# A scatter into an adjacency matrix: two fp16 weight parts instead of three bf16, groups written out, marks in another order

## The chip, the core and the metric

The kernel runs on one core of one Trainium2 chip. A core has five engines with queues of their own: TensorE (PE in the profile, with its weight loads as PEld), VectorE (DVE), ScalarE (ACT), GpSimd (POOL, "PoolE" in the change's words) and SyncE (SP, which issues DMAs). They meet through semaphores alone. The metric is the device time of one launch in microseconds (us); lower is better.

## The reference, cut to what matters

The network works on 625 nodes with 512 features and 20,000 edges that are sorted by destination. Four layers follow each other; the first two need matrices that are made from the edge list:

```python
# layer 0: a weighted graph convolution with self loops of weight 1
deg  = segment_sum(concat([edge_weight, ones(n)]), dst_f)
dinv = where(deg > 0, rsqrt(deg), 0)
agg  = segment_sum(h[src_f] * (dinv[src_f] * w * dinv[dst_f])[:, None], dst_f) + b_conv
# layer 1: a mean over incoming edges; layers 2 and 3: attention over the same edges
agg  = segment_sum(x[src], dst);  mean = agg / maximum(deg, 1)
```

The kernel never gathers rows. It builds, once, a dense matrix of edge counts and one of edge weights (source by destination) and uses them as matmul operands in all layers.

## The kernel before, in words

The node axis is padded to NP = 640, five tiles of 128. The edge list is cut into NG = 40 groups of 512 edges, each group as CH = 4 chunks of 128 edges, one edge to a partition. Since the edges are sorted, a group's destinations fall into a window of WIN = 34 columns (more passes would follow if they did not; the outer loop `Fori(0, passes + 1)` runs once here).

**The stretch before the scatter** loads and transposes the edge lists, finds each group's first destination (`base_f`), normalises x tile by tile (`first_norm`, `first_stats`, `first_rest`) and multiplies it with the first weights (L1838 on PE). `step(...)` on DVE makes the next DVE instruction wait for this one. DVE splits the edge weights into three bf16 parts (`w_part`, L2564 to L2567), whose sum is the float32 weight.

**The scatter**, for each group g, uses buffer b = g % HOT with HOT = 4:

- DVE writes source marks: for chunks 0 to 2, `hot_src[b][:, j]` is 1 where the node number (`iota16`) equals the edge's source, 628 wide (`marks`, L2590). Chunk 3 is made by ACT in two instructions, the distance |node - source| (L1724) and relu(1 - distance) (L1726).
- DVE writes destination marks for all four chunks in one instruction, 4 x 34 wide (L2595), between the second and the third source mark. Its two tensor inputs, `iota16` and `dst_rel` (a part of the tile `edge_col`), are both in SBUF.
- POOL multiplies the destination marks with the three weight parts, 3 x 4 x 34 = 408 wide (L1511).
- PE, for each of 4 chunks and 5 source tiles, loads the 128 source marks as weights and does three matmuls into PSUM: marks and first part together (68 columns, L2134), then the second and third part (34 columns each, L2137). That is 60 matmuls to a group. The increment of `scat_full` tells that the group's sums are there.
- DVE adds the sums into the window of the matrix (`add`, L2605). The window's place comes from `base_i` by a register load on DVE's sequencer (L2601).

DVE's order is hot(g + 3), add(g): it marks three groups ahead. `hot(g + 4)` waits until PE has done group g. The loops over groups are hardware loops (`Fori`) of four groups a turn, on DVE, ACT, POOL and PE, with group numbers in registers. After the scatter DVE sums features (L2642) and the degrees, and ACT and DVE split the matrix into high and low parts (L1729, L2629).

Of the kernel before, what the change touches and what calls it, by code (L numbers as in the profile page):

```python
# [40 lines left out]
ACCW = NP + ROOM  # L41

# [147 lines left out]
def build(nc, a, out):  # L190
    ctx = ExitStack()
    with ctx:
        def sb(name, shape, dt):
            return ctx.enter_context(nc.sbuf_tensor(name, shape, dt))
# [24 lines left out]
        w_part = sb("w_part", [P, 3, CH, NG], BF16)  # L219
        hot_dst = sb("hot_dst", [P, HOT, CH, 4 * ROOM], BF16)  # L220
# [32 lines left out]
        src_col, dst_rel, w_col = [edge_col[:, i * CH * NG:(i + 1) * CH * NG].rearrange("p (j g) -> p j g", j=CH) for i in range(3)]  # L253
        l3s = edge_col[:, 0:5 * NT * NJ].rearrange(
# [27 lines left out]
        hot_src = [m[:, :, :].rearrange("p t n -> p (t n)").bitcast(BF16)[:, b * CH * NP:(b + 1) * CH * NP].rearrange(  # L282
            "p (j n) -> p j n", j=CH) for m in (mask, z) for b in range(2)]
        hot_abs = [mask[:, NT - 1, :].bitcast(BF16)[:, b * NP:(b + 1) * NP] for b in range(2)]
# [1111 lines left out]
        def _(g):  # L1396
# [108 lines left out]
            with g.Fori(0, passes + 1) as kp:  # L1505
                with g.Fori(0, NG // HOT) as gi:
                    for b in range(HOT):
                        gr = gi * HOT + b
                        c = kp * NG + gr + 1
                        g.wait_ge(hot_dst_up, c)  # L1510
                        g.tensor_tensor(hot_dst[:, b, :, WIN:4 * WIN].rearrange("p j (i n) -> p i j n", i=3),  # L1511
                                        hot_dst[:, b, :, 0:WIN].unsqueeze(1).broadcast_to([P, 3, CH, WIN]),
                                        w_part[:, :, :, bass.ds(gr, 1)].broadcast_to([P, 3, CH, WIN]), ALU.mult).then_inc(hot_w_up, 1)
# [157 lines left out]
        def _(act):  # L1671
# [29 lines left out]
            act.activation(diag, ident[:, :].unsqueeze(1).broadcast_to([P, NT - 1, P]), ACT.Copy).then_inc(acc_up, 1)  # L1701
            act.activation(w_acc[:, NT - 1, (NT - 1) * P:NP], ident[:, :], ACT.Copy).then_inc(acc_up, 1)
# [16 lines left out]
            with act.Fori(0, passes + 1) as kp:  # L1719
                with act.Fori(0, NG // HOT) as gi:  # L1720
                    for b in range(HOT):
                        g = gi * HOT + b
                        act.wait_ge(scat_full, kp * NG + g + 1)
                        act.activation(hot_abs[b % 2][:, 0:NW], iota16[:, 0:NW], ACT.Abs, bias=src_col[:, CH - 1, bass.ds(g, 1)], scale=-1.0).then_inc(hot_abs_up, 1)  # L1724
                        act.wait_ge(hot_abs_up, kp * NG + g + 1)
                        act.activation(hot_src[b][:, CH - 1, 0:NW], hot_abs[b % 2][:, 0:NW], ACT.Relu, bias=1.0, scale=-1.0).then_inc(hot_act_up, 1)  # L1726
# [329 lines left out]
        def _(pe):  # L2056
# [8 lines left out]
            pe.matmul(bflat(BIG0["base"])[:, 0:2 * NG], ones[0:NG, :], xn[0:NG, 0, 0:2 * NG],  # L2065
# [53 lines left out]
            with pe.Fori(0, passes + 1) as kp:  # L2119
                with pe.Fori(0, NG // HOT) as gi:  # L2120
                    for b in range(HOT):
# [6 lines left out]
                        for j in range(CH):  # L2128
                            for t in range(NT):
                                s = hot_src[b][:, j, t * P:(t + 1) * P]  # L2130
                                o = t * 2 * WIN


                                pe.matmul(to[:, o:o + 2 * WIN], s, hot_dst[:, b, j, 0:2 * WIN],  # L2134
                                          start=(j == 0 and t == 0), stop=False, skip_group_check=True)
                                for i in (2, 3):
                                    ins = pe.matmul(to[:, o + WIN:o + 2 * WIN], s, hot_dst[:, b, j, i * WIN:(i + 1) * WIN],  # L2137
                                                    start=False, stop=(j == CH - 1 and i == 3), skip_group_check=True)
# [323 lines left out]
        def _(dve):  # L2462
# [33 lines left out]
            step(dve.tensor_scalar(xn[0:NG, 0, NG:2 * NG], ident[0:NG, 0:NG], mnmx[0:NG, 2:3], None, ALU.mult))  # L2496
            def tile_sums(slot, src):
                dve.bn_stats(stats[:, slot, :], src).then_inc(st_up, 1)  # L2498
# [35 lines left out]
            for name, to in (("src", src_col), ("w", w_col)):  # L2534
# [4 lines left out]
            step(dve.tensor_copy(base_f[:, :], bflat(u)[:, 0:NG]))  # L2539
            first_norm(0)  # L2540
# [4 lines left out]
                              base_f[:, :].unsqueeze(1).broadcast_to([P, CH, NG]), ALU.subtract).then_inc(big_read, 1)  # L2545
            first_stats(2)
            first_norm(1)
            dve.wait_ge(big_read, u + 1)
# [15 lines left out]
            step(dve.tensor_copy(w_part[:, 0, :, :], w_col[:, :, :]))  # L2564
            for i in (1, 2):
                step(dve.tensor_tensor(w_col[:, :, :], w_col[:, :, :], w_part[:, i - 1, :, :], ALU.subtract))
                ins = dve.tensor_copy(w_part[:, i, :, :], w_col[:, :, :])  # L2567
                if i == 1:
                    step(ins)
            ins.then_inc(w_ready, 1)  # L2570
# [14 lines left out]
            with dve.Fori(0, passes + 1) as kp:  # L2585
                def hot(g, b):

                    dve.wait_ge(scat_full, kp * NG + g + 1)
                    def marks(j):
                        return dve.tensor_scalar(hot_src[b][:, j, 0:NW], iota16[:, 0:NW], src_col[:, j, bass.ds(g, 1)], None, ALU.is_equal)  # L2590

                    marks(0)
                    marks(1)

                    dve.tensor_tensor(hot_dst[:, b, :, 0:WIN], iota16[:, 0:WIN].unsqueeze(1).broadcast_to([P, CH, WIN]),  # L2595
                                      dst_rel[:, :, bass.ds(g, 1)].broadcast_to([P, CH, WIN]), ALU.is_equal).then_inc(hot_dst_up, 1)
                    marks(2).then_inc(hot_src_up, 1)

                def add(g, b):

                    w0 = dve.value_load(base_i[0:1, bass.ds(g, 1)], min_val=0, max_val=NP)  # L2601
# [3 lines left out]
                    dve.tensor_tensor(win, scat(b).rearrange("p (t c n) -> p t c n", t=NT, c=2), win, ALU.add).then_inc(scat_read, 1)  # L2605
# [3 lines left out]
                for b in range(HOT - 1):  # L2609
                    hot(b, b)  # L2610
                wait_apart(dve, pass_up, kp * 3 + 1)
                with dve.Fori(0, NG // HOT - 1) as gi:
                    for b in range(HOT):
                        hot(gi * HOT + b + HOT - 1, (b + HOT - 1) % HOT)
                        add(gi * HOT + b, b)
                hot(NG - 1, HOT - 1)
                dve.wait_ge(hot_dst_up, kp * NG + NG)
                dve.tensor_scalar(dst_rel[:, :, :], dst_rel[:, :, :], float(WIN), None, ALU.subtract).then_inc(pass_up, 1)
                dve.tensor_scalar(base_f[0:1, :], base_f[0:1, :], float(WIN), float(NP), ALU.add, ALU.min).then_inc(pass_up, 1)
                for b in range(HOT):  # L2620
                    add(NG - HOT + b, b)
# [34 lines left out]
            dve.tensor_scalar(degs[:, 0, :], degree, 1.0, None, ALU.add).then_inc(deg_up, 1)  # L2656
# [161 lines left out]
```

## Time and profile before

| | |
|---|---|
| median of 3 runs | 871.7 us (870.86 to 872.49) |
| the profiled execution | 873.27 us, of which the span of its instructions is 871.3 us |
| busy, share of the span | PE 95%, PEld 83%, DVE 72%, POOL 57%, ACT 53% |
| granted TensorE clock, mean | 0.994 |
| before the scatter (0 to 28.07 us) | 28.07 us |
| the scatter (DVE's first mark to the end of its last add) | 28.07 to 102.83 us |
| all that follows | 768.47 us |

All numbers below come from this one profiled execution, and times of instructions are counted from the span's start. The busy share of PE counts overlapping matmuls of some 190 ns that start every 28 ns, so it tells little here; starts tell more. An instruction can start before the recorded end of the one ahead of it on its engine.

### The profile page before, as it was taken

The page shows a single profiled execution, that of the slowest core. Times are in us where ns is not written, and L with a number is a line of the kernel's source. Part 1 is how long each engine was busy: PE and PEld are TensorE (multiplying, and loading weights), DVE is VectorE, ACT ScalarE, POOL GpSimd, SP SyncE. Part 2 cuts the span into 40 slices and gives each one's busy share as a digit, 9 for nine tenths or more (in the row PEclk, how much of TensorE's full clock was granted, in tenths as well). Part 3 has the DMA queues.
Part 4 walks back from the last instruction along what each step waited for, and adds up shares of the span by engine and source line. Part 5 has one row for each costly group of instructions (what it writes and reads, how often), then busy time and mean ns, then how long its engine had stood idle before and what let it go on. Part 6 is the DMA issues. An engine that isn't in the chain of part 4 may idle for free.

```text
span 871.3 us, 18208 instructions
## 1 busy us (share of the span) xinstructions
PE 823.4 (95%) x6778; PEld 725.1 (83%) x6778; DVE 628.2 (72%) x1271; ACT 458.2 (53%) x773; POOL 494.3 (57%) x542
## 2 busy tenths in 40 slices
PE   3999989999999999999999999999999999999896
PEld 2999867889998879999887989887998978875565
DVE  7998878974676673576766467677348766699996
ACT  5988675344771343575233467333347633256673
POOL 7454573578433577542556943266674339457971
PEclk9999999999999999999999999999999999989999
DMA  6000102133000152200124410014230003100111
GB/s 163 2 0 0 38 25 87 41 94 122 25 1 13 41 158 73 72 14 1 29 68 126 110 49 2 13 31 121 86 95 13 1 1 85 37 1 32 48 60 60
DMA packets 49761, 44.34 MB, mean 51 GB/s; under 512 B 6014, under 2 KB 37440, under 8 KB 49699
## 3 DMA queue, kind: packets, MB, share of 16 engines
q1 hardware_dynamic: 47234, 39.72, 15.7%
q10 hardware_dynamic: 2464, 3.80, 1.6%
q8 instruction: 38, 0.62, 0.3%
q14 instruction: 25, 0.20, 0.1%
HBM read 42.04 MB, written 1.33 MB: 50 GB/s over the span
## 4 chain that ended last, share of the span: by engine, by line
PE 73%; DVE 15%; ACT 4%; issue 3%; DMA 2%; DVEq 1%; POOL 1%; SPq 0%; ACTq 0%
PE psum L1832 20%; PE psum L1943 13%; PE psum L1838 12%; PE psum L1996 8%; PE psum L1862 6%; PE psum L1913 6%; PE psum L2137 2%; DVE arena L1026 2%; PE psum L2134 2%; PE psum L948 2%; PE psum L1886 2%; PE psum L890 1%; DVE stats L2498 1%; DVE arena L2374 1%; DMA x<-in_x 1%
## 5 line engine op out<-in xcount | busy, mean ns | idle before, releaser
L1373 POOL TENSOR_SCALAR acc<-acc,rden,flag 128x628 f32<-128x628 f32 x80 | 69.8, 873 | 105.3 <-DVE rden L2370 105.3
L1943 PE MATMUL psum<-ringw,arena 128*128 128x512 f32 (+1 forms) x480 | 119.5, 398 | 4.1 <-DVE arena L2382 2.5
L1832 PE MATMUL psum<-arena,ringw 128*128 128x314 f32 x768 | 114.3, 310 | 0.1
L1832 PEld LDWEIGHTS psum<-arena,ringw 128*128 128x128 f32 x768 | 113.0, 190 | 1.4 <-DVE arena L2347 1.1
L1943 PEld LDWEIGHTS psum<-ringw,arena 128*128 128x128 f32 (+1 forms) x480 | 86.8, 186 | 25.8 <-DVE arena L2382 3.5
L2374 DVE TENSOR_TENSOR arena<-psum,arena 128x640 fp32r<-128x640 f32 x80 | 65.7, 821 | 36.2 <-ACT arena L1631 36.2
L1832 PE MATMUL psum<-arena 128*128 128x314 f32 (+1 forms) x480 | 87.4, 320 | 2.6 <-DVE arena L2374 2.1
L1996 PE MATMUL psum<-arena 128*128 128x384 f32 (+3 forms) x480 | 82.4, 311 | 0.0
L1444 POOL TENSOR_TENSOR ringw<-raw,ringw 128x512 fp32r<-128x512 f32 x56 | 71.8, 1292 | 15.4 <-ACT ringw L1675 15.4
L2347 DVE SCALAR_TENSOR_TENSOR arena<-psum,cols,arena 128x628 fp32r<-128x628 f32 x32 | 27.9, 872 | 72.4 <-ACT arena L1613 72.4
L1862 PE MATMUL psum<-ident,acc 128*128 128x128 f32 (+1 forms) x528 | 76.2, 273 | 0.1
L1832 PEld LDWEIGHTS psum<-arena 128*128 128x128 f32 (+1 forms) x480 | 70.6, 187 | 6.6 <-DVE arena L2374 4.6
L1996 PEld LDWEIGHTS psum<-arena 128*128 128x128 f32 (+1 forms) x480 | 74.3, 189 | 0.6
L1444 POOL TENSOR_TENSOR ringw<-xn,ringw 128x512 fp32r<-128x512 f32 x49 | 65.4, 1340 | 16.3 <-ACT ringw L1675 16.3
L1631 ACT ACTIVATE arena<-psum 128x640 fp32r<-128x640 f32 x80 | 56.4, 705 | 33.8 <-PE psum L1862 32.4
L1626 ACT ACTIVATE acc<-acc,nsmax 128x628 f32<-128x628 f32 x80 | 65.1, 814 | 9.4 <-DVE nsmax L2365 9.0
L1862 PEld LDWEIGHTS psum<-ident,acc 128*128 128x128 f32 (+1 forms) x528 | 62.0, 139 | 7.9 <-DVE arena L2347 1.1
L2365 DVE CUSTOM_DVE_ANT_0 acc<-psum,mask 128x628 f32<-128x628 f32 x80 | 63.8, 802 | 0.0
L1562 ACT ACTIVATE arena<-psum 128x512 fp32r<-128x512 f32 x40 | 23.8, 595 | 75.5 <-PE psum L1862 60.4
L1437 POOL TENSOR_SCALAR veps<-mv 128x1 f32<-128x1 f32 x60 | 13.7, 229 | 87.7 <-DVE mv L2502 85.8
L1838 PE MATMUL psum<-arena,ringw 128*128 128x314 f32 x384 | 58.4, 310 | 2.3 <-DVE arena L2264 2.3
L1913 PE MATMUL psum<-ringw,arena 128*128 128x512 f32 x240 | 58.7, 395 | 0.9 <-DVE arena L2264 0.6
(315 smaller groups left out, 1922.5 us busy)
## 6 DMA issues: line engine op xcount, KB each, us to landing
raw<-in_L_gnn_m_w SPq DMA_DIRECT2D x16, 256.0 KB
xn<-in_L_gnn_m_w SPq DMA_DIRECT2D x16, 256.0 KB
raw<-in_L_gnn_wv SPq DMA_DIRECT2D x8, 256.0 KB
xn<-in_L_gnn_wv SPq DMA_DIRECT2D x8, 256.0 KB
raw<-in_L_gnn_wq SPq DMA_DIRECT2D x8, 256.0 KB
xn<-in_L_gnn_wq SPq DMA_DIRECT2D x8, 256.0 KB
raw<-in_L_gnn_wk SPq DMA_DIRECT2D x8, 256.0 KB
xn<-in_L_gnn_wk SPq DMA_DIRECT2D x8, 256.0 KB
```

What stands on the lines that cost most here:

```text
L1373: g.tensor_scalar(pbuf[:, k % 4, 0:NW], pbuf[:, k % 4, 0:NW], rden[:, k:k + 1], flag[:, 1, k % NT:k % NT + 1], ALU.mult, ALU.mult).then_in ...
L1444: g.tensor_tensor(to[1], place(n), to[0].bitcast(F32), ALU.subtract).then_inc(split_done, 1)
L1626: act.activation(pbuf[:, k % 4, 0:NW], pbuf[:, k % 4, 0:NW], ACT.Exp, bias=nsmax[:, k:k + 1], scale=-1.0, accum_out=den[:, k:k + 1]).then_ ...
L1631: act.activation(pT[:, 0, :, (k % NT) * P:(k % NT + 1) * P], bflat(u).rearrange("p (k n) -> p k n", k=NT), ACT.Copy).then_inc(phi_up, 1)
L1832: ins = pe.matmul(big[buf(u)][0:l.shape[1], h, 0:HW], l, r[:, h * HW:(h + 1) * HW], start=(i == 0), stop=(i == len(terms) - 1))
L1838: ins = pe.matmul(to, l, r, start=(i == 0), stop=(i == len(terms) - 1))
L1862: ins = pe.transpose(bflat(u)[0:KEYS[k], k * P:(k + 1) * P], src[:, k * P:k * P + KEYS[k]], ident[:, :])
L1913: ins = pe.matmul(brow(u), l, r, start=(k == 0 and i == 0), stop=(k == KT - 1 and i == 2))
L1943: ins = pe.matmul(brow(ROWBLK[f"{name}{t}"])[0:KEYS[t], :], l, r, start=(pieces[0] + i == 0), stop=(pieces[-1] == KT - 1 and i == len(term ...
L1996: ins = pe.matmul(head_sums(name, at.stop - at.start), l, r, start=(st == 0 and i == 0), stop=(st == NT - 1 and i == len(terms) - 1))
L2365: dve.tensor_tensor_reduce(wide(pbuf[:, k % 4, :]), bwide(u), wide(mask[:, t, :]), -DH ** -0.5, 3e38, ALU.add, ALU.min, nsmax[:, k:k + 1]) ...
L2374: dve.tensor_tensor(pT[:, 1, :, t * P:(t + 1) * P], bflat(u).rearrange("p (k n) -> p k n", k=NT), f32(pT[:, 0, :, t * P:(t + 1) * P]), ALU ...
```

## The change

There are five edits.

1. The weights are scaled by a power of two and split into two fp16 parts instead of three bf16 ones. The scale `w_one` comes from the largest weight (a reduction, a PE product, four small DVE steps) and goes into the diagonal's ones and the degree too. Marks and parts are fp16. The scale of a destination's column drops out later, with the degree.
2. PE does two matmuls instead of three on each loaded weight tile: 40 to a group. POOL's product is 2 x 4 x 34 = 272 wide.
3. The groups are written out on DVE and ACT: no inner hardware loop, fixed addresses and group numbers there. PE and POOL keep their loops.
4. DVE's order in a group: destination marks first, then the three source marks; the register load of the add's window stands ahead of the next group's marks. ACT makes the distances one group ahead, with a third buffer.
5. POOL's product also waits for `hot_src_up`, which the last of DVE's source marks increments.

```diff
-        w_part = sb("w_part", [P, 3, CH, NG], BF16)
-        hot_dst = sb("hot_dst", [P, HOT, CH, 4 * ROOM], BF16)
+        w_part = sb("w_part", [P, 2, CH, NG], F16)
+        w_unit = sb("w_unit", [P, 3], F32)
+        hot_dst = sb("hot_dst", [P, HOT, CH, 4 * ROOM], F16)
...
                         g.wait_ge(hot_dst_up, c)
-                        g.tensor_tensor(hot_dst[:, b, :, WIN:4 * WIN].rearrange("p j (i n) -> p i j n", i=3),
+                        g.wait_ge(hot_src_up, c)
+                        g.tensor_tensor(hot_dst[:, b, :, WIN:3 * WIN].rearrange("p j (i n) -> p i j n", i=2),
...
+            act.wait_ge(dstep, W_ONE_STEP)
+            act.activation(diag, ident[:, :].unsqueeze(1).broadcast_to([P, NT - 1, P]), ACT.Copy, scale=w_one).then_inc(acc_up, 1)
...
+                act.wait_ge(scat_full, kp * NG + HOT)
+                distances(0)
+                for g in range(NG):
+                    if g + 1 < NG:
+                        distances(g + 1)
+                    act.wait_ge(scat_full, kp * NG + g + 1)
+                    act.wait_ge(hot_abs_up, kp * NG + g + 1)
+                    act.activation(hot_src[g % HOT][:, CH - 1, 0:NW], hot_abs[g % 3][:, 0:NW], ACT.Relu, ...)
...
-                                for i in (2, 3):
-                                    ins = pe.matmul(to[:, o + WIN:o + 2 * WIN], s, hot_dst[:, b, j, i * WIN:(i + 1) * WIN],
+                                ins = pe.matmul(to[:, o + WIN:o + 2 * WIN], s, hot_dst[:, b, j, 2 * WIN:3 * WIN],
...
+            step(dve.tensor_reduce(xn[0:NG, 0, 2 * NG:2 * NG + 2], edge[0:NG, 2, :]..., AX.X, ALU.max,
...
-            step(dve.tensor_copy(w_part[:, 0, :, :], w_col[:, :, :]))
-            for i in (1, 2):
-                step(dve.tensor_tensor(w_col[:, :, :], w_col[:, :, :], w_part[:, i - 1, :, :], ALU.subtract))
...
+            step(dve.tensor_scalar(w_part[:, 0, :, :], w_col[:, :, :], w_one, None, ALU.mult))
+            dve.scalar_tensor_tensor(w_part[:, 1, :, :], w_col[:, :, :], w_one, w_part[:, 0, :, :], ALU.mult, ALU.subtract).then_inc(w_ready, 1)
...
+                    dve.tensor_tensor(hot_dst[:, b, :, 0:WIN], iota16[:, 0:WIN]..., dst_rel[:, :, g:g + 1]..., ALU.is_equal).then_inc(hot_dst_up, 1)
                     marks(0)
                     marks(1)
                     marks(2).then_inc(hot_src_up, 1)
...
+                for g in range(NG):
+                    w0 = window(g)
+                    if g + HOT - 1 < NG:
+                        hot(g + HOT - 1)
...
+                    add(g, w0)
```

On DVE, in the middle of the scatter, one group stands like this before (L2590 source mark, L2595 destination marks, L2601 the window's register load, L2605 the add; ISA and REGISTER_ALU are the sequencer's own):

```order
L2590 ISA [waits scat_full]
L2590 TENSOR_SCALAR mask<-iota16,edge_col 128x628
L2590 ISA
L2590 TENSOR_SCALAR mask<-iota16,edge_col 128x628
L2595 ISA
L2595 TENSOR_TENSOR hot_dst<-iota16,edge_col 128x4x34
L2590 ISA
L2590 TENSOR_SCALAR mask<-iota16,edge_col 128x628
L2601 ISA
L2601 TENSOR_LOAD base_i
L2601 ISA x2
L2602 ISA
```

And at the same place after the change (L2605 is now the destination marks, L2603 the source marks, L2613 the register load, L2619 the add):

```order
L2613 TENSOR_LOAD base_i
L2613 ISA x2
L2605 TENSOR_TENSOR hot_dst<-iota16,edge_col 128x4x34 [waits scat_full]
L2603 TENSOR_SCALAR mask<-iota16,edge_col 128x628 x3
L2616 REGISTER_ALU
L2619 ISA [waits scat_read,scat_full]
L2619 TENSOR_TENSOR acc<-psum,acc 128x10x34
```

The destination marks moved from behind two source marks to directly behind the add of the group before, the three source marks stand together, and the register load moved ahead of them all.

On POOL, one group of the scatter after the change (L1515 is the product, which was L1511 and waited for hot_dst_up alone):

```order
L1513 ISA
L1515 ISA [waits hot_src_up,hot_dst_up]
L1515 TENSOR_TENSOR hot_dst<-hot_dst,w_part 128x2x4x34
L1513 ISA
L1515 ISA [waits hot_src_up,hot_dst_up]
```

The product is released by the last source mark, no longer by the destination marks.

On DVE, in the stretch before the scatter, behind the copies of sources and weights (L2549 and L2552 copies from PSUM, L2524 and L2511 normalise a tile of x and take its sums):

```order
L2552 COPY base_f<-psum 128x40 [waits big_full]
L2553 TENSOR_REDUCE w_unit<-psum 128x1 [waits dstep]
L2524 TENSOR_SCALAR xn<-x,mv,rstd 128x512 [waits rstd_up,dstep]
L2555 TENSOR_REDUCE span<-psum 128x1
L2558 TENSOR_TENSOR edge_col<-psum,base_f 128x160 [waits big_full]
L2560 TENSOR_SCALAR w_unit<-w_unit 128x1
L2511 BN_STATS stats<-x 128x6 [waits dstep]
L2515 BN_AGGR mv<-stats 128x2 [waits st_up]
L2562 TENSOR_SCALAR w_unit<-w_unit 128x1
L2524 TENSOR_SCALAR xn<-x,mv,rstd 128x512 [waits rstd_up,dstep]
L2564 TENSOR_SCALAR w_unit<-w_unit 128x1
```

The four instructions on w_unit (L2553, L2560, L2562, L2564) are new there.

## Rows read from the trace of the kernel before

**Rows 1.** Stretch, its us, then busy us (count): PE, PEld, DVE, ACT, POOL; clock, DMA.
```profile
28.07:102.83 74.76, 73.19 (x2425) 70.81 (x2423) 69.61 (x203) 61.19 (x81) 39.12 (x43) 1.00 0.01 4
```
**Rows 2.** Timeline, PE: start us, us, engine, line, operation, out<-in, shapes, count.
```profile
44.40 0.19 PE L2134 MATMUL psum<-hot_dst,z 128*128 128x68 bf16 x1
...
44.77 0.19 PE L2134 MATMUL psum<-hot_dst,mask 128*128 128x68 bf16 x1
```
**Rows 3.** Timeline, PE, inside a group.
```profile
42.73 0.19 PE L2134 MATMUL psum<-hot_dst,z 128*128 128x68 bf16 x1
...
42.81 0.19 PE L2134 MATMUL psum<-hot_dst,z 128*128 128x68 bf16 x1
```
**Rows 4.** Timeline, DVE, from an add to the next.
```profile
41.39 0.50 DVE L2605 TENSOR_TENSOR acc<-psum,acc 128x340 f32 x1
41.81 0.90 DVE L2590 TENSOR_SCALAR mask<-iota,edge_col 128x628 bf16<-128x628 f16 x2
42.64 0.29 DVE L2595 TENSOR_TENSOR hot_dst<-iota,edge_col 128x136 bf16<-128x136 f16 x1
42.85 0.37 DVE L2590 TENSOR_SCALAR mask<-iota,edge_col 128x628 bf16<-128x628 f16 x1
43.14 0.50 DVE L2605 TENSOR_TENSOR acc<-psum,acc 128x340 f32 x1
```
**Rows 5.** Timeline, DVE, two source marks later in the scatter.
```profile
64.73 0.67 DVE L2590 TENSOR_SCALAR mask<-iota,edge_col 128x628 bf16<-128x628 f16 x2
```
**Rows 6.** Timeline, POOL, one product.
```profile
43.10 0.89 POOL L1511 TENSOR_TENSOR hot_dst<-hot_dst,w_part 128x408 bf16<-128x408 bf16 x1 [0.85 <-DVE hot_dst L2595]
```
**Rows 7.** Groups of POOL instructions by shape: count | busy us, mean ns | idle before.
```profile
L1444 POOL TENSOR_TENSOR ringw<-raw,ringw 128x512 fp32r<-128x512 f32 x56 | 71.8, 1292 | 15.4 <-ACT ringw L1675 15.4
...
L616 POOL TENSOR_TENSOR arena<-hot_dst,arena 128x64 fp32r<-128x64 f32 x1 | 0.3, 313 | 0.0
L624 POOL TENSOR_TENSOR arena<-ident 16x8 fp32r<-16x8 f32 x1 | 0.2, 198 | 0.0
```
**Rows 8.** Timeline, DVE and POOL, far behind the scatter.
```profile
783.01 1.52 POOL L649 TENSOR_TENSOR hot_dst<-hot_dst,acc 128x628 f32<-128x628 f32 x1
...
783.70 0.86 DVE L1035 TENSOR_TENSOR edge_col<-edge_col 128x10 f32<-128x10 f32 x1
784.59 0.17 DVE L1037 SCALAR_TENSOR_TENSOR edge_col<-edge_col 128x10 f32<-128x10 f32 x1
```
**Rows 9.** Timeline, DVE, third source marks of groups 0, 3 and 39, and the end.
```profile
28.87 0.38 DVE L2590 TENSOR_SCALAR mask<-iota,edge_col 128x628 bf16<-128x628 f16 x1
...
34.12 0.37 DVE L2590 TENSOR_SCALAR z<-iota,edge_col 128x628 bf16<-128x628 f16 x1
...
98.23 0.37 DVE L2590 TENSOR_SCALAR z<-iota,edge_col 128x628 bf16<-128x628 f16 x1
...
102.32 0.51 DVE L2605 TENSOR_TENSOR acc<-psum,acc 128x340 f32 x1 [0.75 <-PE psum L2137]
```
**Rows 10.** Timeline, DVE and POOL, before the scatter.
```profile
14.95 0.15 DVE L2550 CAST span_i<-span 128x1 int32<-128x1 f32 x1
15.14 0.15 DVE L2551 TENSOR_SCALAR span_i<-span_i 128x1 int32<-128x1 int32 x1
...
16.31 1.26 POOL L1444 TENSOR_TENSOR ringw<-raw,ringw 128x512 fp32r<-128x512 f32 x1
...
16.49 1.17 DVE L2557 TENSOR_SCALAR arena<-ones,cols 128x128 fp32r<-128x128 f32 x1
...
22.05 0.23 DVE L2564 CAST w_part<-edge_col 128x160 bf16<-128x160 f32 x1
...
23.47 0.69 DVE L2574 TENSOR_TENSOR bias<-psum,bias 128x512 f32<-128x512 f32 x1
...
24.67 0.54 DVE L2511 TENSOR_SCALAR xn<-x,mv,rstd 128x512 f32<-128x512 f32 x1
```
**Rows 11.** Busy time late in the kernel; columns as in the first group.
```profile
776.00:780.00 4.00, 2.68 (x10) 1.69 (x10) 3.98 (x8) 1.45 (x3) 2.97 (x2) 0.86 0.00 0
```

More of the change, by code:

```diff
@@ L1719, in _, with distances @@
             with act.Fori(0, passes + 1) as kp:
[L1720 to L1726, printed above, removed]
+                def distances(g):
+                    if g >= 3:
+                        act.wait_ge(hot_act_up, kp * NG + g - 2)
+                    act.activation(hot_abs[g % 3][:, 0:NW], iota16[:, 0:NW], ACT.Abs, bias=src_col[:, CH - 1, g:g + 1], scale=-1.0).then_inc(hot_abs_up, 1)
+                act.wait_ge(scat_full, kp * NG + HOT)
[5 more added lines that the diff above has]
+                    act.wait_ge(hot_abs_up, kp * NG + g + 1)
+                    act.activation(hot_src[g % HOT][:, CH - 1, 0:NW], hot_abs[g % 3][:, 0:NW], ACT.Relu, bias=1.0, scale=-1.0).then_inc(hot_act_up, 1)
             wait_apart(act, scat_read, (passes + 1) * NG + HOT)
@@ L2064, in _ @@
             pe.wait_ge(dstep, 9)
[L2065 removed]
+            pe.wait_ge(dstep, 10)
+            pe.matmul(bflat(BIG0["base"])[:, 0:2 * NG + 2], ones[0:NG, :], xn[0:NG, 0, 0:2 * NG + 2],
                       start=True, stop=True).then_inc(big_full, 1)
@@ L2539, in _ @@
             step(dve.tensor_copy(base_f[:, :], bflat(u)[:, 0:NG]))
+            step(dve.tensor_reduce(w_unit[:, 0:1], bflat(u)[:, 2 * NG:2 * NG + 2], AX.X, ALU.add))
             first_norm(0)
@@ L2545, in _ @@
                               base_f[:, :].unsqueeze(1).broadcast_to([P, CH, NG]), ALU.subtract).then_inc(big_read, 1)
+            step(dve.tensor_scalar(w_unit[:, 0:1], w_unit[:, 0:1], 2.0 ** -100, None, ALU.max))
             first_stats(2)
+            step(dve.tensor_scalar(w_unit[:, 1:2].bitcast(I32), w_unit[:, 0:1].bitcast(I32), 23, None, ALU.arith_shift_right))
             first_norm(1)
+            step(dve.tensor_scalar(w_one.bitcast(I32), w_unit[:, 1:2].bitcast(I32), float(-2 ** 23), float(268 * 2 ** 23), ALU.mult, ALU.add))
+            assert own[0] == W_ONE_STEP
             dve.wait_ge(big_read, u + 1)
@@ L2655, in _ @@
             dve.wait_ge(deg_full, 1)
-            dve.tensor_scalar(degs[:, 0, :], degree, 1.0, None, ALU.add).then_inc(deg_up, 1)
+            dve.tensor_scalar(degs[:, 0, :], degree, w_one, None, ALU.add).then_inc(deg_up, 1)
             dve.wait_ge(deg_up, 1)
```

55 lines of the change are left out of this document (25 added, 30 removed).

## The prediction

> **What bounds the kernel now.** I read the busy times by stage first. The scatter takes 74.76 us of the span, with the TensorE clock at full rate all the way and DMA at 1% [rows 1]; nothing else in the kernel is touched but the 28 us ahead of it. So the prediction is the length of one group's turn times 40, and a few ends.
>
> The timeline of PE comes next. Inside a group a set of three matmuls takes 83 ns (42.73 to 42.81) [rows 3], so 20 sets take 1.67 us. At the turn of PE's hardware loop, once in four groups, PE starts nothing from about 44.48 (44.40 and its set) to 44.77 [rows 2]: some 0.3 us, and nobody is waited for. From the third source mark of group 3 to that of group 39 the distance is 98.23 - 34.12 = 64.11 us [rows 9], or 1.78 us a group: PE's 1.67 and about 0.1 for loop turns.
>
> The timeline of DVE shows that two more things are as long. From one add to the next there are 43.14 - 41.39 = 1.75 us [rows 4]. In it the pair of source marks behind the add takes 0.90, but 0.67 at 64.73 [rows 4, 5]. The difference is POOL: its product runs from 43.10 to 43.99 [rows 6], and the mark that starts at 43.56 by the same pattern isn't finished before that. The turn closes on itself: destination marks end (42.64 + 0.29 = 42.93), POOL starts 0.17 later, runs 0.89, the held source mark ends, and the next destination marks follow. Three limits of 1.75 to 1.78 stand side by side, so to take away PE's share alone would bring almost nothing; all three are touched, and the question is what the new turn is.
>
> **The prices.** *PE.* Two matmuls on each weight tile instead of three: 20 x 2 x 28 ns = 1.12 us by the starts in [rows 3], and 0.1 for the loop turns: 1.2 us. Not below 1.12; and 1.78 if all stays.
>
> *POOL's product.* 272 elements are not shown. Of the two-input products, 8 elements take 198 ns, 64 take 313 and 512 take 1292 [rows 7], so a fixed part of about 0.18 us and 2.2 ns an element. The bf16 product of 408 takes 0.89: (0.89 - 0.18) / 408 = 1.74 ns an element. With these two, 0.18 + 272 x 1.74 ns = 0.655 us, my value, since it is the row of the same instruction. Low end: all of it shrinks, 0.89 x 2/3 = 0.595. High end: fp16 is handled at the float32 price, 0.18 + 272 x 2.2 = 0.77; if nothing shrinks, 0.89.
>
> *DVE's order, with nobody in the way.* A source mark to the next instruction: 0.295 (0.67 for two, of which the second takes 0.37) [rows 5]; destination marks to the next: 42.85 - 42.64 = 0.21; an add to the next: 41.81 - 41.39 = 0.42 [rows 4]. A turn is 3 x 0.295 + 0.21 + 0.42 = 1.52 us. The register load that stood between is off this path by its new place, and the written-out groups need fewer register instructions, so I count DVE's sequencer as hidden behind these 1.5 us.
>
> *The new order against POOL.* This decides. POOL now starts 0.17 after the end of the third source mark, that is 0.37 + 0.17 = 0.54 after that mark's start. By then DVE is in the add (0.295 to 0.72). The add reads PSUM and one SBUF tile, and stays at 0.50 although POOL runs beside it (43.14 against 43.10) [rows 4, 6]. But the next instruction is no longer a source mark, it is the destination marks, with both inputs in SBUF, and POOL's product still has some 0.5 us to go. Whether POOL holds such an instruction is seen far behind the scatter: POOL's product of 783.01 ends at 784.53; DVE's L1035 of ten elements with both inputs in SBUF starts at 783.70 and takes 0.86 instead of the 0.17 of its like at 784.59, and ends at 784.56 [rows 8]. So it is held until POOL ends and is done 0.03 later, having saved 0.14 of its own 0.17. The destination marks should end 0.29 - 0.14 = 0.15 after POOL. Then the first source mark starts 0.08 before that end (0.29 - 0.21), and the second and third 0.295 behind each other.
>
> The turn, from third source mark to third source mark: 0.54 + 0.655 + 0.15 - 0.08 + 2 x 0.295 = 1.855 us. The add costs nothing (under POOL), and neither do PE's 1.2 us nor ACT: its two marks were 61.19 us busy for 40 groups, 1.53 a group with no overlap between the two [rows 1]. PE, ACT and DVE all come free by this and the turn is set by DVE and POOL alternating, since the wait that was added puts the product behind all three source marks.
>
> The GPSIMD Engine Reference of the Trainium skill (section Key points) speaks against this change in the same way: GpSimd shares its SBUF interfaces with VectorE, and contends with instructions in a two-port mode or with two SBUF inputs. All rows here that show the second kind are float32; the rule makes no such condition. The VectorE: DVE Perf Modes page (The DRAIN you can't avoid) says that a next operation doesn't start until the pipe is empty; by it three overlaps of 0.08 would go and the turn would be 2.1 us. The trace disagrees: instructions start 0.08 before the end of the one ahead [rows 5], so I don't use it.
>
> *Ahead of the scatter.* The new reduction of 40 x 512 falls before the wait for x. The four small steps cost 15.14 - 14.95 = 0.19 each [rows 10], 0.77 in all, before DVE reaches L2557. That one is held anyway: it starts at 16.49 and lasts 1.17, until POOL's product of 16.31 is over at 17.57 [rows 10]. Arriving at 17.26 it ends at the same time; nothing is lost, and 0.8 would be if that cover went. Behind it the splitting of weights took 23.47 - 22.05 = 1.42 us, five instructions; now two, about 0.23 and 0.33: 0.86 less before the last tile is normalised at 24.67 [rows 10]. PE was busy with products nearly until that tile came, so I give 0.2 us to it. Sum -0.2 (0.6 either way as bounds).
>
> *The ends of the scatter.* Groups 0 to 3 are marked with no add between. There POOL collides with a source mark: the turn is about 0.54 + 0.13 (POOL waits for the mark in progress) + 0.655 + 0.18 - 0.08 = 1.43, at most 1.6, where it was (34.12 - 28.87) / 3 = 1.75 [rows 9]: -1.0 (down to -0.5). From the third mark of group 39 to the end: before 102.83 - 98.23 = 4.6 [rows 9]; after, POOL's end (1.3), then three adds at some 0.8 each of register load and wait, and 0.5: 4.0. That is -0.6.
>
> **Sum.** 36 turns x (1.855 - 1.78) = +2.7; start of the scatter -1.0; its end -0.6; ahead of it -0.2: +0.9 us. Against the profiled execution's 873.27 that gives 874.2; this execution lies 1.6 above the median, so 871.7 + 0.9 = 872.6 us. The case's own range: the product at 0.595 gives 36 x -0.06 = -2.2, at 0.77 +4.1, the rest +-0.6: 870 to 877.
>
> **Rivals.**
> *A. The destination marks aren't held* (their inputs are an fp16 tile and a small float32 one, both repeated, and no row shows such an instruction beside POOL). Then the turn is DVE's own 1.52, or 1.545 with the first source mark waiting for POOL's end: 36 x (1.545 - 1.78) = -8.5, with the ends -1.8: -10.3, so 861.4 us. For it: nothing but that gap in the rows; against it [rows 8].
> *B. The fp16 product is dearer* than 0.63 us, from which point on the whole is no gain. At 0.77 the time is 877; at 0.89 it is +0.235 x 36 = 8.5 more, 881. POOL is on the path of each turn now, so every 0.1 us of it is 3.6 us.
> *C. TensorE's clock falls.* PE will stand still 0.7 us of each 1.86. The clock was full throughout the scatter [rows 1], and fell to half late in the kernel in a stretch where PE was busy 2.68 us of 4 [rows 11]. If matmuls took twice as long, a group's 40 would take 2.24 us and bind: 36 x 0.46 = +17, about 888. Below a doubling of 1.65 it hides.
> *D. The removed work was not on the path and nothing else moves*: PE's third matmul goes, the turn stays 1.75 by DVE's sequencer: -1 for the turns, -1 for the ends, 870. It is inside the first case's range.
>
> **Chances.** Forecast with its range 0.62 (with D); A 0.16; B beyond 877 0.10; C 0.06; something not seen here 0.06. A measurement of this kernel tells about 0.2% (1.7 us) from no change. Faster by more: A, and 0.1 of the first case and a part of the unseen, 0.26. Slower by more: B, C, and about a quarter of the first case, 0.34. Within: 0.40. The range runs from A to the lower part of B: 860.8 to 877.5, which leaves out some 0.16; the likeliest case's own is 870 to 877.
>
> **What would show it.** In the new profile: PE's pairs at 56 ns, and PE idle before each group, released by POOL or DVE; destination marks of about 0.63 us instead of 0.29 (from 0.72 behind the third source mark's start to 0.15 behind POOL's end at 1.2); source marks never above 0.38 in the middle; POOL's product near 0.66; a turn of 1.85. If the destination marks stay at 0.29 while POOL runs, the held instruction of the new order is wrong and A holds. If POOL's product isn't 0.6 to 0.7, B or its reverse. If the instruction that was L2557 ends later than 17.66, the stretch ahead wasn't covered.

## The result and the profile after

| | before | after |
|---|---|---|
| median, runs on the same chip | 872.16 us (5 runs, 870.86 to 872.53) | 876.13 us (5 runs, 875.49 to 877.05) |
| ratio, 95% interval | | 1.005 (1.0038 to 1.0061) |
| the profiled execution, its span | 873.27, 871.3 us | 877.05, 875.3 us |

The change makes the kernel 0.5% slower, by 4.0 us. That is more than the 0.2% that a measurement of this kernel can tell. The time is inside the range given, on its slower side, 3.5 us above the value given.

The busy times of the scatter's stretch answer to [rows 1], and a stretch of it, and the late stretch of [rows 11], stand below them (stretch, its us, busy us and count of PE, PEld, DVE, ACT, POOL, then clock and DMA):

```profile
28.07:102.83 74.76, 55.62 (x1571) 52.63 (x1570) 74.76 (x198) 56.43 (x81) 25.84 (x39) 0.95 0.00 1
52.40:55.80 3.40, 3.34 (x78) 3.20 (x75) 3.40 (x10) 1.90 (x4) 1.31 (x2) 0.50 0.00 0
...
776.00:780.00 4.00, 3.61 (x25) 2.91 (x24) 3.87 (x11) 2.38 (x5) 1.29 (x1) 1.00 0.00 0
```

PE went from 73.19 busy us to 55.62, POOL from 39.12 to 25.84, and DVE from 69.61 to every moment of the stretch. DVE is the bound now. The late fall of the clock has only moved along with the rest (it begins at 782.8 instead of 778.9). But a share of 100% is not 100% work, as the timeline of DVE shows (it answers to [rows 4, 5]):

```profile
60.35 0.50 DVE L2619 TENSOR_TENSOR acc<-psum,acc 128x340 f32 x1
60.77 0.70 DVE L2605 TENSOR_TENSOR hot_dst<-iota,edge_col 128x136 f16<-128x136 f16 x1
61.40 0.96 DVE L2603 TENSOR_SCALAR z<-iota,edge_col 128x628 f16<-128x628 f16 x3
62.27 0.50 DVE L2619 TENSOR_TENSOR acc<-psum,acc 128x340 f32 x1
62.70 0.70 DVE L2605 TENSOR_TENSOR hot_dst<-iota,edge_col 128x136 f16<-128x136 f16 x1
```

and the timeline of POOL for the same time (it answers to [rows 6]):

```profile
60.66 0.66 POOL L1515 TENSOR_TENSOR hot_dst<-hot_dst,w_part 128x272 f16<-128x272 f16 x1 [1.27 <-DVE mask L2603]
62.59 0.65 POOL L1515 TENSOR_TENSOR hot_dst<-hot_dst,w_part 128x272 f16<-128x272 f16 x1 [1.27 <-DVE z L2603]
```

Read them together. The three source marks end at 61.40 + 0.96 = 62.36. POOL's product starts at 62.59 and ends at 63.24. The destination marks start at 62.70, have 0.29 us of work, and are entered as 0.70: they end at 63.40, 0.16 behind POOL. The add between (62.27, 0.50) is not lengthened. From add to add there are now 1.92 us, where there were 1.75 in the stretch shown before. All 40 destination marks and all 40 products, by their two lines (duration min/median/max in ns, first and last start):

```profile
L2605 DVE TENSOR_TENSOR hot_dst<-iota,edge_col x40: 287/698/704, 27.9 to 101.1; 128x136 f16<-128x136 f16 x40
```
```profile
L1514 POOLq EVENT_SEMAPHORE  x40: 17/17/17, 29.1 to 102.7; - x40
...
L1515 POOLq FUSED_REGOPS  x40: 42/42/42, 29.1 to 102.8; - x40
L1515 POOL TENSOR_TENSOR hot_dst<-hot_dst,w_part x40: 651/652/783, 29.3 to 102.9; 128x272 f16<-128x272 f16 x40
```

PE has slack. Its sets of two are 0.06 us apart (they answer to [rows 3]), and it waits for POOL's product before a group:

```profile
61.57 0.19 PE L2146 MATMUL psum<-hot_dst,mask 128*128 128x68 f16 x1 [0.38 <-POOL hot_dst L1515]
61.60 0.18 PE L2148 MATMUL psum<-hot_dst,mask 128*128 128x34 f16 x1
61.63 0.19 PE L2146 MATMUL psum<-hot_dst,mask 128*128 128x68 f16 x1
```

The start and the end of the scatter on DVE answer to [rows 9] (x3 are the three source marks of a group; the third starts 0.37 before their end), and the instruction that was L2557, now L2575, to [rows 10]:

```profile
17.05 0.34 DVE L2575 TENSOR_SCALAR arena<-ones,cols 128x128 fp32r<-128x128 f32 x1
...
28.09 0.96 DVE L2603 TENSOR_SCALAR mask<-iota,edge_col 128x628 f16<-128x628 f16 x3
...
32.17 1.36 DVE L2603 TENSOR_SCALAR z<-iota,edge_col 128x628 f16<-128x628 f16 x3
...
101.74 0.96 DVE L2603 TENSOR_SCALAR z<-iota,edge_col 128x628 f16<-128x628 f16 x3
...
105.33 0.51 DVE L2619 TENSOR_TENSOR acc<-psum,acc 128x340 f32 x1 [0.38 <-PE psum L2148]
```

The third source marks of groups 0, 3 and 39 start at 28.68, 33.16 and 102.33, where they stood at 28.87, 34.12 and 98.23. So the path to the end of the last add, 105.84 instead of 102.83, is: ahead of the scatter -0.2; groups 0 to 3, 4.48 instead of 5.25: -0.8; 36 turns, 69.17 instead of 64.11: +5.05, or 1.921 a turn instead of 1.781; the end, 3.5 instead of 4.6: -1.1. Sum +3.0. The remaining 1.0 us of the 4.0 arises behind the scatter, and most of it has a cause of its own (below).

### The profile page after: what moved, and what is told of

Its sections match the earlier page's. It is cut to its first block, busy times and chain, and to the rows that moved or that the text cites. A ratio compares the mean times of both kernels' runs of the same rounds, so it can differ in the third digit from the quotient of the medians.

```text
span 875.3 us, 16395 instructions
## 1 busy us (share of the span) xinstructions
PE 809.1 (92%) x5978; PEld 709.5 (81%) x5978; DVE 635.5 (73%) x1272; ACT 453.4 (52%) x773; POOL 484.2 (55%) x542
## 4 chain that ended last, share of the span: by engine, by line
PE 68%; DVE 17%; issue 4%; ACT 4%; POOL 3%; SPq 2%; DMA 1%; DVEq 1%; POOLq 0%; ACTq 0%
PE psum L1843 20%; PE psum L1954 11%; PE psum L1849 10%; PE psum L2007 8%; PE psum L1873 6%; PE psum L1924 5%; DVE arena L1029 2%; PE psum L951 2%; PE psum L2146 2%; PE psum L1897 1%; DVE z L2603 1%; PE psum L893 1%; POOL hot_dst L1515 1%; DVE mask L2603 1%; DVE stats L2511 1%
## 5 line engine op out<-in xcount | busy, mean ns | idle before, releaser
L1447 POOL TENSOR_TENSOR ringw<-raw,ringw 128x512 fp32r<-128x512 f32 x56 | 71.8, 1293 | 15.3 <-ACT ringw L1679 15.3
L1447 POOL TENSOR_TENSOR ringw<-xn,ringw 128x512 fp32r<-128x512 f32 x49 | 65.3, 1338 | 16.7 <-ACT ringw L1679 16.7
```

Of the source, the lines that this page charges most:

```text
L1447: g.tensor_tensor(to[1], place(n), to[0].bitcast(F32), ALU.subtract).then_inc(split_done, 1)
```

## The experiments

Seven kernels ran, four and then three, each time with the kernel before on the same chip: its median was 871.5 and 871.9 us (21 runs each). The turn is told as the distance of adds, averaged over groups 0 to 35.

| kernel | marks' order | product | waits | turn | median us | ratio, 95% interval |
|---|---|---|---|---|---|---|
| before | 2 source, dst, source | 408 | dst | 1.788 | 871.5; 871.9 | 1 |
| after | dst, 3 source | 272 | dst, source | 1.921 | 876.13 | 1.005 (1.0038 to 1.0061) |
| old place | as before | 272 | dst | 1.509 | 861.79 | 0.989 (0.9874 to 0.9904) |
| no hold | as after | 272 | dst | 1.925 | 882.60 | 1.012 (1.0108 to 1.0139) |
| one wait | as after | 272 | source | 1.862 | 873.37 | 1.002 (1.0009 to 1.0027) |
| old place, hold | as before | 272 | source | 1.802 | 871.67 | 1.000 (0.9996 to 1.0015) |
| two parts only | as before, in loops | 272 | dst | 1.787 | 873.01 | 1.001 (1.0004 to 1.0022) |
| written out only | as before | 408 | dst | 1.745 | 871.77 | 1.000 (0.9993 to 1.0011) |
| wide product | as after | 408 | dst, source | 2.157 | 885.25 | 1.016 (1.0146 to 1.0177) |

### The destination marks back in their old place, no hold

Against the changed kernel:

```diff
-                        g.wait_ge(hot_src_up, c)
...
-                    dve.tensor_tensor(hot_dst[:, b, :, 0:WIN], ..., ALU.is_equal).then_inc(hot_dst_up, 1)
                     marks(0)
                     marks(1)
+                    dve.tensor_tensor(hot_dst[:, b, :, 0:WIN], ..., ALU.is_equal).then_inc(hot_dst_up, 1)
                     marks(2).then_inc(hot_src_up, 1)
```

> The changed kernel with two edits undone: the destination marks stand between the second and the third source mark again, and GpSimd's product waits for the destination marks alone. Theory (the destination marks, with two SBUF inputs, are held by GpSimd's product, which the added wait put behind all source marks): the product (0.65 us) now ends before DVE comes to the next first source mark, so nothing is held and DVE's own turn binds: 3 x 0.295 + 0.21 + 0.42 = 1.52 us instead of the 1.92 of the changed kernel. 36 x 0.40 = 14.4 us less: about 862 us, 10 below the kernel before. Rival 1 (the written-out groups cost VectorE or ScalarE something in each turn, such as the fetching of code): the turn stays above 1.8 and the time near 876. Rival 2 (TensorE's waits set the turn): no change either, 876.

Measured: 861.79 us, a ratio of 0.989 to before. DVE and POOL in its trace:

```profile
60.75 0.50 DVE L2618 TENSOR_TENSOR acc<-psum,acc 128x340 f32 x1
61.17 0.67 DVE L2602 TENSOR_SCALAR z<-iota,edge_col 128x628 f16<-128x628 f16 x2
61.75 0.29 DVE L2606 TENSOR_TENSOR hot_dst<-iota,edge_col 128x136 f16<-128x136 f16 x1
61.96 0.38 DVE L2602 TENSOR_SCALAR z<-iota,edge_col 128x628 f16<-128x628 f16 x1
62.26 0.50 DVE L2618 TENSOR_TENSOR acc<-psum,acc 128x340 f32 x1
```
```profile
60.71 0.66 POOL L1514 TENSOR_TENSOR hot_dst<-hot_dst,w_part 128x272 f16<-128x272 f16 x1 [0.85 <-DVE hot_dst L2606]
```

The product starts with the add and ends at 61.37, when the first source mark has run 0.2 of its 0.37 us. Most of it falls under the add, which it doesn't hold, and its end comes early enough for the mark: no instruction is lengthened, and the turn is the 1.51 us of DVE's own work. This is the fastest version of the case: 10 us less than the kernel before. It keeps the first three edits and the rest of the fourth (the early register load, ACT one group ahead), and together they are a gain; the place of the destination marks and the hold turn it into a loss of 4.

### The new order without the hold

Against the changed kernel:

```diff
                         g.wait_ge(hot_dst_up, c)
-                        g.wait_ge(hot_src_up, c)
```

> The changed kernel with one edit undone: GpSimd's product waits for the destination marks alone, which stay first. Theory (it is the place of the product among DVE's held instructions that counts, not the wait as such): the product starts 0.17 us behind the destination marks, beside the first source mark, and the second source mark is held until its end. Turn: 0.29 + 0.17 + 0.65 + 0.18 - 0.08 + 0.295 (third mark, add) + 0.42 = 1.93 us, as now (1.92): 876 us, within 1.5. Rival (the added wait alone is the cost, and without it the product is hidden): turn 1.52, 862 us.

Measured: 882.6 us. The turn came as expected, 1.925 us. Here the product of 0.65 runs against the source marks:

```profile
60.03 0.28 DVE L2604 TENSOR_TENSOR hot_dst<-iota,edge_col 128x136 f16<-128x136 f16 x1
60.24 1.38 DVE L2602 TENSOR_SCALAR mask<-iota,edge_col 128x628 f16<-128x628 f16 x3
61.53 0.50 DVE L2618 TENSOR_TENSOR acc<-psum,acc 128x340 f32 x1
```

The three marks take 1.38 instead of 0.96. So in the new order the product costs 0.4 whether it is held back or not: with the hold it lengthens the destination marks (0.70 for 0.29), without it the source marks. The total was missed by 6.6 us, and not in the turn. At the end of the scatter POOL goes on to products of another kind (L1447, then L1497, 1.3 us each). In the changed kernel they start at the same time (103.54), but there the hold has let DVE finish its last source marks at 102.70. Here DVE is still in them, and its last steps are held one after the other:

```profile
103.45 2.65 POOL L1447 TENSOR_TENSOR ringw<-raw,ringw 128x512 fp32r<-128x512 f32 x2
```
```profile
102.59 2.38 DVE L2602 TENSOR_SCALAR z<-iota,edge_col 128x628 f16<-128x628 f16 x3
104.89 1.30 DVE L2631 TENSOR_SCALAR edge_col<-edge_col 128x160 f32<-128x160 f32 x1
106.12 1.25 DVE L2632 TENSOR_SCALAR base_f<-base_f 1x40 f32<-1x40 f32 x1
```

In the changed kernel the last two take 0.23 and 0.17. The last add ends at 110.27 instead of 105.84, which is 4.4 of the 6.5 us between the two kernels. During and behind the pause in PE's work the granted clock is at half (104.7 to 108.1 and 111.5 to 118.4), and the next stage takes 2.1 us more than in the changed kernel (columns as above):

```profile
96.00:103.00 7.00, 4.91 (x151) 4.58 (x152) 7.00 (x20) 1.23 (x2) 2.13 (x4) 1.00 0.00 1
103.00:106.00 3.00, 1.40 (x39) 1.29 (x35) 3.00 (x3) 0.00 (x0) 3.00 (x3) 0.79 0.08 4
106.00:110.00 4.00, 2.56 (x26) 1.89 (x23) 3.04 (x6) 0.00 (x0) 1.33 (x2) 0.73 0.45 128
110.00:118.00 8.00, 7.58 (x25) 5.93 (x26) 7.45 (x18) 6.89 (x14) 2.33 (x3) 0.60 0.12 33
```

So the hold isn't worthless in the new order: it doesn't shorten the turn, but it orders the end.

### The hold by one wait

The last source mark is behind the destination marks on DVE, so its semaphore alone is enough. Against the changed kernel:

```diff
-                        g.wait_ge(hot_dst_up, c)
                         g.wait_ge(hot_src_up, c)
```

> The changed kernel, but GpSimd waits for the last source mark alone (which comes behind the destination marks on the same engine), in one instruction instead of two. Theory (the product starts 0.235 us behind the last source mark's end, not the 0.17 of the kernel before, because GpSimd's sequencer now runs two waits): 0.06 us off each of 36 turns, turn 1.86, -2.3 us: 873.9 us. Rival (the longer start has another cause, such as the port or the kind of the operand): the start stays at 0.235 and the time at 876.1.

Measured: 873.37 us, turn 1.862. The three source marks, and POOL's product with its idle time before:

```profile
60.74 0.96 DVE L2602 TENSOR_SCALAR z<-iota,edge_col 128x628 f16<-128x628 f16 x3
```
```profile
61.87 0.65 POOL L1514 TENSOR_TENSOR hot_dst<-hot_dst,w_part 128x272 f16<-128x272 f16 x1 [1.21 <-DVE z L2602]
```

The product starts 61.87 - 61.70 = 0.17 behind the last mark's end, where it was 62.59 - 62.36 = 0.23, and the idle time is 1.21 instead of 1.27. The second wait is a sequencer instruction of its own on POOL (L1514 in the lines of the changed kernel), and costs 0.06 us between the last source mark and the product; in the new order that is on the path of each of the 36 turns. The last add ends 1.9 us earlier than in the changed kernel (103.92 instead of 105.84); the runs don't tell where the rest of the 2.8 us between the medians arises.

### The old place with the hold

Against the changed kernel:

```diff
-                        g.wait_ge(hot_dst_up, c)
                         g.wait_ge(hot_src_up, c)
...
-                    dve.tensor_tensor(hot_dst[:, b, :, 0:WIN], ..., ALU.is_equal).then_inc(hot_dst_up, 1)
                     marks(0)
                     marks(1)
+                    dve.tensor_tensor(hot_dst[:, b, :, 0:WIN], ..., ALU.is_equal).then_inc(hot_dst_up, 1)
```

> The changed kernel with the destination marks in their old place, between the second and third source mark, and GpSimd's product still held until the last source mark, by one wait. Theory: the product ends in the middle of the next first source mark, which is held until 0.18 us behind it: turn 0.37 + 0.17 + 0.65 + 0.18 - 0.08 + 0.295 + 0.21 = 1.80 us, -0.12 x 36 = -4.4 against the changed kernel: 871.7 us. Rival (the hold costs nothing once the destination marks have moved back): 1.52, 862 us.

Measured: 871.67 us, turn 1.802. The product starts 0.3 us later than in the first experiment and now reaches into the first source mark:

```profile
60.40 0.50 DVE L2618 TENSOR_TENSOR acc<-psum,acc 128x340 f32 x1
60.82 0.96 DVE L2602 TENSOR_SCALAR z<-iota,edge_col 128x628 f16<-128x628 f16 x2
61.70 0.29 DVE L2606 TENSOR_TENSOR hot_dst<-iota,edge_col 128x136 f16<-128x136 f16 x1
```

Two source marks take 0.96 instead of 0.67. The hold costs 0.29 of a turn in the old place, all of the gain. The new place costs another 0.06 behind it, the second wait 0.06 more.

### The two fp16 parts alone

Against the kernel before, edits 1 and 2:

```diff
+        w_part = sb("w_part", [P, 2, CH, NG], F16)
+        hot_dst = sb("hot_dst", [P, HOT, CH, 4 * ROOM], F16)
...
+                                ins = pe.matmul(to[:, o + WIN:o + 2 * WIN], s, hot_dst[:, b, j, 2 * WIN:3 * WIN], ...)
```

> The kernel before with the first two edits alone: two fp16 weight parts (PE two matmuls a tile pair less, POOL's product 272 wide), while DVE's and ScalarE's groups stay in their hardware loops, the destination marks stay between the second and third source mark, and the product waits for them alone. My theory: before, three limits stood side by side near 1.78 us a turn: PE's matmuls (1.67 and the loop's pause), the registers that DVE's sequencer loads inside the loop (adds 1.75 us apart where no wait shows), and DVE's own work at 1.52. Taking PE's work away alone leaves the sequencer's: turns of 1.745 to 1.75 us, 36 x (1.75 - 1.78) = -1.1 us, about 870.5 us. Rival, PE was the only bound of the turn: turns of 1.53 us, 36 x -0.25 = -9 us, about 862.5 us. By either the product takes about 0.66 us and the PE pairs 56 ns.

Measured: 873.01 us, not faster than before, so PE's matmuls were not the only bound and that rival fell. (L2596 is the source mark here, L2611 the add.) But my number was missed too: the turn is 1.72 to 1.75 three times out of four and 2.08 the fourth time (HOT = 4 groups are one turn of the loop), 1.825 on average from 44 us on. DVE, across one of these:

```profile
59.78 0.38 DVE L2596 TENSOR_SCALAR z<-iota,edge_col 128x628 f16<-128x628 f16 x1
60.27 0.51 DVE L2611 TENSOR_TENSOR acc<-psum,acc 128x340 f32 x1
60.90 0.68 DVE L2596 TENSOR_SCALAR z<-iota,edge_col 128x628 f16<-128x628 f16 x2
...
62.35 0.51 DVE L2611 TENSOR_TENSOR acc<-psum,acc 128x340 f32 x1 [0.27 <-PE psum L2141]
```

No instruction is lengthened by POOL here, but the add starts 0.49 behind the third mark's start, where it needs 0.295 with the groups written out. Once in four groups the next mark also starts 0.63 behind the add instead of 0.42, and the next add waits for PE although PE is busy only 40.1 us of 55. So DVE's looped groups with their register loads bind, together with the pauses at the loops' turns on other engines, of which the runs don't tell the shares. The kernel before shows the same pattern of 1.75, 1.75, 1.72 and 2.08 from 62 us on. The pattern was in the trace that I predicted from; I quoted the 1.75 of the first half and the average, and put the rest down to PE's pause. The 1.1 us over the kernel before lie behind the scatter: in this trace the last add ends 0.2 us earlier, 0.7 is lost right behind it, where the clock is at half from 104.7 to 108.1, and 1.3 at SyncE's issue, told below (this execution lies 1.9 us above its kernel's median).

### The groups written out alone

Against the kernel before, edit 3, and from edit 4 the register load and ACT's distances one group ahead:

```diff
-                with dve.Fori(0, NG // HOT - 1) as gi:
+                for g in range(NG):
+                    w0 = window(g)
+                    if g + HOT - 1 < NG:
+                        hot(g + HOT - 1)
...
+                    add(g, w0)
```

> The kernel before with the third edit alone: groups written out on DVE with the window's registers loaded one group ahead, ScalarE one group ahead, but three bf16 weight parts, the old place of the destination marks and no hold on the product. My theory: PE's 3 matmuls a tile (83 ns a set) still take 1.67 us a turn and with the loop's pause 1.78, so nothing changes: turns of 1.78 us, about 871.5 us (870.5 to 873). Rival, DVE's sequencer was the only bound: turns of 1.52 us, 36 x -0.26 = -9.4 us, about 862 us. If this one and the kernel with the two parts alone both stay near 871, while the kernel with both edits in the old order took 861.8, the gain belongs to neither edit alone.

Measured: 871.77 us; the time is as expected, and so is PE's part in it. The adds are an even 1.745 apart, and DVE has no free moment between them:

```profile
60.75 0.50 DVE L2612 TENSOR_TENSOR acc<-psum,acc 128x340 f32 x1
61.17 0.90 DVE L2596 TENSOR_SCALAR z<-iota,edge_col 128x628 bf16<-128x628 f16 x2
61.99 0.29 DVE L2600 TENSOR_TENSOR hot_dst<-iota,edge_col 128x136 bf16<-128x136 f16 x1
```

What sets this distance is the product of 0.89, which holds the first source mark until 61.6, the closed turn that the prediction described for [rows 4, 6]. But PE is slower still. Its loop turns once in four groups, and the first matmuls behind two turns are

```profile
59.42 0.19 PE L2140 MATMUL psum<-hot_dst,mask 128*128 128x68 bf16 x1
...
66.59 0.19 PE L2140 MATMUL psum<-hot_dst,mask 128*128 128x68 bf16 x1
```

They are 7.17 us apart, for four groups, or 1.79 for one, and between 31 and 102 us PE waits for nobody. So PE falls behind DVE by some 0.05 us a group, and at the end the last adds wait for it (1.67 apart; the last ends at 102.97, before it was 102.83). PE's matmuls bind this kernel, and they bound the kernel before as well (the first matmul behind the turn ahead of these lines starts at 44.77 [rows 2]):

```profile
45.00 0.22 PE L2137 MATMUL psum<-hot_dst,mask 128*128 128x34 bf16 x2
...
51.95 0.19 PE L2134 MATMUL psum<-hot_dst,mask 128*128 128x68 bf16 x1
```

From 44.77 to 51.95 there are again 7.18 us for four groups, and from 31 to 102 us PE waits 0.2 us in all. So neither edit alone gains: with the matmuls gone the looped groups bind (7.30 us for four), with the loops gone the matmuls do (7.17). Together in the old order they gain 10 us, for the narrower product also takes the first source mark out of POOL's way (0.24 us of DVE's turn).

### The product wide again, in the new order

Against the changed kernel, with the product 408 wide:

```diff
+        w_part = sb("w_part", [P, 3, CH, NG], F16)
+            g.memset(w_part[:, 2, :, :], 0.0).then_inc(hot_init, 1)
...
+                        g.tensor_tensor(hot_dst[:, b, :, WIN:4 * WIN]..., ALU.mult).then_inc(hot_w_up, 1)
```

> The changed kernel, with a third weight part of zeros that PoolE multiplies as well: its product is 408 columns wide again and takes 0.89 us instead of 0.65, and nobody reads the third block, so nothing else is different. My theory: in the changed order the product lies whole on each turn (last source mark's end, product, destination marks' end, two source marks), so every turn gets 0.24 us longer: 1.92 + 0.24 = 2.16 us, 36 x 0.24 = +8.6 us, about 885 us (883 to 887). Rival, the product only overlaps work that DVE has anyway, and the turn is set by DVE's own instructions being dear in this order: the time stays at 876 us. A third, half of it shows (+4 us), if the destination marks run part of the way beside the product.

Measured: 885.25 us, turn 2.157. The turn rose by the whole 0.24 us of the product, 36 x 0.236 = 8.5 us, and the last add ends 8.8 us later (114.63); the medians are 9.1 apart:

```profile
62.02 0.94 DVE L2606 TENSOR_TENSOR hot_dst<-iota,edge_col 128x136 f16<-128x136 f16 x1
```

The destination marks are 0.94 long for the same 0.29 us of work. In the new order the product lies whole on the path.

## Why the prediction was right, and where it wasn't

The direction, the range and the mechanism held. The value given did not say much: +0.9 us would have been no measurable change, and +4.0 is a clear loss, to which the chances had given 0.34.

**The turn.** The mechanism is shown: the destination marks were held behind POOL and ended 0.16 after it (0.15 was given), source marks stayed at 0.37, the add was free, the product took 0.652 (0.655). The experiment with the wide product confirms that it is on every turn, and the old place removes the hold altogether. One term was mis-sized: POOL's start behind the third source mark, 0.17 by the kernel before, where the product had one wait. It is 0.23, since the edit adds a wait and not only moves one. The experiment with one wait shows it: 1.862 us against the 1.855 of the sum. 36 x 0.066 = 2.4 us, most of the 3.5 that were missing (1.0 more is SyncE's issue, 0.5 the median of the kernel before in these runs, and the ends give 0.3 back). I had counted what is queued behind the new wait, and not the wait's own instruction.

**The kernel before.** The prediction had three limits side by side at 1.75 to 1.78 and PE's at 1.67 + 0.1. Its reading of [rows 2] took the pause at PE's loop turn as 0.3 us; a second one of 0.23 follows it (44.77 to 45.00), so PE's turn is 1.79, and PE never waited for DVE. DVE's own limit was not one number either: 1.745 by the held mark up to 60 us, 1.825 by the loops from 62 us on. The sum goes by the measured 64.11 us of 36 turns, so this error didn't enter it.

**The ends.** Groups 0 to 3 took 4.48 where 4.3 was given, the end 3.5 where 4.0 was given; both errors are small and of opposite sign. Ahead of the scatter 0.2 was right. L2557's successor ends at 17.39 and was held by nothing; the bound of 17.66 holds.

**Behind the scatter.** I had written that nothing else is touched. 1.0 us came from there. Laid beside the trace of before, instruction by instruction from the last add on, DVE runs 0.35 us late up to 605 us and 1.2 from 610 us on: 0.87 us arise there. A DMA-issuing row of SyncE's queue, of before and then of after:

```profile
591.93 1.88 SPq L1262 DMA_DIRECT2D xn<-in_L_gnn_s_w  x4
```
```profile
595.30 2.92 SPq L1265 DMA_DIRECT2D xn<-in_L_gnn_s_w  x4
```

The third of these four issues takes 1.50 us instead of 0.42, the transfers behind it leave later, and ScalarE waits 3.6 us for a weight block where it waited 2.5. The DMA queues of the microsecond 595 to 596 in the trace of after (packets, MB, share of 16 engines) show a packet that carries instructions:

```profile
q8 instruction: 1, 0.02, 8.7%
```

The long issue (1.06 to 1.90 us) is there in all seven traces with the two fp16 parts, at this third issue of the third pass each time, and each time with a packet of instructions that starts between 0.25 us ahead of its start and 0.17 behind it. All nine traces have another such packet 1.7 to 2.0 us ahead of it. In before and in the kernel with the groups written out alone that one is the nearest, and the issue takes 0.42. The latter loses nothing against before between 605 and 610 us; the seven others lose 0.4 to 1.9 us there. So the kernels with edits 1 and 2 have a loading of the program at a transfer that is waited for. That the one causes the other is only argued: no run moved the packet by itself.

**The rivals.** A (not held) is refuted for the new order, and the 861.4 that it gave is near what the old order takes (861.8). Its mechanism, a product that holds nothing, is the old order's; that the numbers agree so well is in part luck, since its turn was 1.545 and the measured one is 1.509. B (a dearer product) fell at 0.652. C happened in part: the clock is at half from 52.4 to 55.8 and from 83.1 to 86.5, and PE does 78 matmuls in the first of them, some 44 ns each instead of 28, or 1.74 us for a group's 40. That is still under the 1.92 of the turn, and the adds stay 1.92 apart there, so it cost nothing; I had taken their time to double (2.24). D's 870 was inside the range; the two parts alone in their loops took 873.

The GPSIMD Engine Reference of the Trainium skill (Key points), by which GpSimd contends with VectorE instructions that have two SBUF inputs, holds here for fp16 and float32 inputs as well: 0.29 became 0.70. The trace agrees with the rule, and adds that the held instruction ends only 0.16 us behind the product. The Trainium skill's page VectorE: DVE Perf Modes (The DRAIN you can't avoid) gave the prediction a turn of 2.1 by its sentence that the next operation doesn't start until the pipe is empty. The same paragraph of the page adds that a next operation which isn't held starts earlier, which the prediction passed over. The trace agrees with the addition: the turn is 1.92, and starts are still 0.08 before the end of the instruction ahead (61.40 against 60.77 + 0.70, and 0.96 for three marks of 0.37).

## What to carry to other kernels

When POOL and DVE alternate, lay POOL's product beside the DVE instruction that it doesn't hold (here the add that reads PSUM), and check in the timeline that it ends before the next one that it does hold: 0.3 us of delay in its start cost the whole gain of 10 us. A busy share of 100% can hide held instructions, so compare the same instruction's duration in two places. Where several limits stand side by side, price them together; and count each added wait as an instruction of its own on its sequencer.

## What the hardware showed that I had not expected

- A second semaphore wait ahead of a POOL instruction costs 0.06 us of its start (0.23 against 0.17 behind the last source mark).
- A single-input float32 DVE instruction of one partition and 40 elements is held until a POOL product of 1.3 us is over (L2632 of the kernel with no hold: 1.25 instead of 0.17).
- In the changed kernel the clock falls to half for 3.4 us in two places of the scatter, with PE idle about a quarter of the time (55.62 busy us of 74.76), and comes back; with PE busy 73.19 us of the same length it never fell. More idle time alone doesn't tell when: during the even turns it never fell in the kernels with turns of 1.80, 1.86 and 1.925 us (old place with the hold, one wait, no hold), and in the scatter of the one with 2.16 it fell six times. In no kernel did such a fall lengthen a turn.
- The clock's fall at 779 us of the kernel before lasts 6.8 us. In three traces (old place, written out only, wide product) the same fall lasts 3.4 us, and they gain 1.5 to 1.8 us there on the trace of before. The runs don't show why, so the tail of a single trace is no measure of a change in the scatter.
- An issue of a DMA on SyncE took up to 1.9 us instead of 0.42 where a packet of instructions began within 0.25 us of its start.
